# Score product of a cross-attention kernel: high and low part of a head's q on the two halves of the partitions, four products of 154 columns in place of three of 308

## The reference

```
q = layernorm(x) @ Wq            # (4, 16 heads, 1024, 64)
k, v = ctx @ Wk, ctx @ Wv        # (4, 16 heads, 154, 64)
attn = softmax(q k^T * SCALE)    # (4, 16, 1024, 154)
x = x + (attn v) @ Wo + bo
h = silu(fp4(n) @ fp4(w_gate)^T) * (fp4(n) @ fp4(w_up)^T)   # n = layernorm(x), 704 wide
x = x + fp4(h) @ fp4(w_down)^T
```

## Time and profile before

| | |
|---|---|
| Time, median of 3 runs | 921.65 us (921.07 to 922.3) |
| Profiled execution, its own time | 919.93 us |
| Its span | 918.1 us, so 1.8 us lie around it |
| Mean granted clock of TensorE | 0.982 of full speed |
| Instructions | 21443 |

### The profile page before, as it was taken

How to read it: one execution, slowest core, us unless ns; L and a number is a source line. 1 busy time by engine, 2 the same in 40 slices (tenths; PEclk the granted TensorE clock), 3 DMA queues, 4 the chain that set the end, 5 groups by cost and what they waited for, 6 DMA issues and landing times.

```text
span 918.1 us, 21443 instructions
## 1 busy us (share of the span) xinstructions
PE 839.2 (91%) x6254; PEld 801.2 (87%) x6254; DVE 707.2 (77%) x2140; ACT 524.1 (57%) x1879; POOL 544.5 (59%) x811
## 2 busy tenths in 40 slices
PE   3787899999999999989999999989999999999964
PEld 3676889999989999989988999989988999999863
DVE  5678788878777888868777888877877888887863
ACT  4554566566665556556665665656655665655521
POOL 6438577666455666654545666656554666666662
PEclk9999999999999999999999999999999999999986
DMA  7110000001010000001010000001000000000000
GB/s 239 47 28 28 7 19 13 24 13 41 14 42 13 13 25 12 23 11 47 7 36 24 7 25 12 23 16 42 13 13 19 14 24 13 14 10 12 13 6 11
DMA packets 20151, 23.22 MB, mean 25 GB/s; under 512 B 2658, under 2 KB 18250, under 8 KB 20042
## 3 DMA queue, kind: packets, MB, share of 16 engines
q1 hardware_dynamic: 20042, 21.94, 7.6%
HBM read 17.74 MB, written 4.19 MB: 24 GB/s over the span
## 4 chain that ended last, share of the span: by engine, by line
PE 64%; DVE 21%; issue 6%; ACT 5%; POOL 2%; DVEq 0%; POOLq 0%; ACTq 0%
PE ps_q L985 10%; PE ps_g L1067 9%; PE ps_s L1027 8%; PE ps_t L1037 6%; PE ps_o L1052 5%; PE ps_o L1050 5%; PE ps_o L1051 5%; DVE negmax L826 3%; DVE pT_lo L679 3%; PE ps_g L948 3%; PE ps_m L1079 3%; DVE scales L706 3%; PE ps_m L1081 2%; PE ps_m L1080 2%; PE ps_m L913 2%
## 5 line engine op out<-in xcount | busy, mean ns | idle before, releaser
L492 POOL TENSOR_TENSOR probs<-probs,rsum 128x308 f32<-128x308 f32 x256 | 180.3, 705 | 266.5 <-DVE rsum L790 259.1
L650 ACT ACTIVATE probs<-ps_s,negmax 128x154 f32<-128x154 f32 x512 | 194.7, 386 | 222.1 <-DVE negmax L826 221.0
L826 DVE TENSOR_REDUCE negmax<-ps_s 128x2 f32<-128x308 f32 x256 | 120.9, 472 | 89.0 <-PE ps_s L1027 88.4
L1050 PE MATMUL ps_o<-B_sb,pT_lo 128*128 128x256 f32 x640 | 180.5, 282 | 0.6 <-DVE x_both L881 0.6
L1052 PE MATMUL ps_o<-B_sb,pT_hi 128*128 128x256 f32 x640 | 180.4, 282 | 0.0
L1051 PE MATMUL ps_o<-B_sb,pT_hi 128*128 128x256 f32 x640 | 180.0, 281 | 0.0
L679 DVE TENSOR_TENSOR pT_lo<-ps_t,pT_hi 128x256 fp32r<-128x256 f32 (+1 forms) x256 | 122.7, 479 | 34.8 <-ACT pT_hi L544 34.3
L1067 PE MATMUL ps_g<-WGU,xqT_hi 128*128 128x352 f32 x512 | 135.5, 346 | 3.6 <-DVE B_sb L679 1.9
L1037 PE MATMUL ps_t<-ident,probs 128*128 128x128 f32 x640 | 113.8, 276 | 25.3 <-DVE pT_lo L679 22.5
L1050 PEld LDWEIGHTS ps_o<-B_sb,pT_lo 128*128 128x128 f32 x640 | 120.7, 189 | 0.9 <-issue 0.8
L1052 PEld LDWEIGHTS ps_o<-B_sb,pT_hi 128*128 128x128 f32 x640 | 121.0, 189 | 0.0
(11 more groups left out here) (157 smaller groups left out, 2198.1 us busy)
## 6 DMA issues: line engine op xcount, KB each, us to landing
xa<-in_x_dram SPq DMA_DIRECT2D x33, 128.0 KB, 2.1
xr<-in_x_dram SPq DMA_DIRECT2D x32, 128.0 KB, 2.0
out_dram<-y_xn SPq DMA_DIRECT2D x32, 128.0 KB, 1.7
W_sb<-in_L_xattn_Wk_dram SPq DMA_DIRECT2D x4, 512.0 KB, 3.6
W_sb<-in_L_xattn_Wv_dram SPq DMA_DIRECT2D x3, 512.0 KB, 3.6
probs<-in_L_xattn_Wq_dram SPq DMA_DIRECT2D x2, 512.0 KB, 7.8
Wo_sb<-in_L_xattn_Wo_dram SPq DMA_DIRECT2D x1, 1024.0 KB, 8.9
VT<-in_L_ffn_w_down_dram SPq DMA_DIRECT2D x2, 352.0 KB, 3.9
```

Source lines behind the costliest of these rows:

```text
L492: pool.tensor_tensor(unit, unit, rsum[:, 2 * u:2 * u + 2].unsqueeze(2) .to_broadcast([P, 2, M]), ALU.mult).then_inc(norm_p, 1)
L650: ins = act.activation(probs[:, h, 0:M], ps_s[k % 2][:, s * M:(s + 1) * M], ACT.Exp, bias=negmax[:, h:h + 1], accum_out=sums[:, h:h + 1])
L826: dve.tensor_reduce(negmax[:, 2 * k:2 * k + 2], ps_s[k % 2][:, 0:UM].rearrange("p (h m) -> p h m", h=2), AX_X, ALU.max, negate=True).then_ ...
L1050: pe.matmul(ps_o[:, 0:C], lo[:, j, :], w[:, 0:C], start=first, stop=False)
```

## The change

The low and the high part of q come to lie in one tile, q_sb[128, units, 2 heads, 256]. For head s, its high part is on its own 64 partitions (`mine`) and its low part on the other 64 (`other`). K's high part is written on both halves of the partitions, and K's low part on the head's own half with zeros on the other. A contraction over 128 partitions then gives q_hi x K_hi + q_lo x K_hi with K_sb[0], and q_hi x K_lo with K_sb[1], for one head and 154 columns. Per unit there are two heads and two such products, hence four matmuls, each with its own 128-column stationary operand.

```
-            pool.memset(K_sb[0][:, :, :].bitcast(F32), 0.0).then_inc(kpad_p, 1)
...
             def q_hi_part(pair, u):
-                hi_part(q_sb[0][:, u, :], ps_q[:, 0:2 * P], (q_mm, PAIRS * pair + u + 1), q_hi)
+                act.wait_ge(q_mm, PAIRS * pair + u + 1)
+                for s in range(2):
+                    ins = act.activation(q_sb[mine(s), u, s, :], ps_q[mine(s), 0:2 * P], ACT.Copy)
+                ins.then_inc(q_hi, 1)
...
                 if kind == "K":
                     act.wait_ge(k_mm, KV * b + i + 1)
-                    if isinstance(b, int) and i == 0:
-                        act.wait_ge(kpad_p, 2)
-                    for s in range(2):
-                        h = slice(D * s, D * s + D)
-                        ins = act.activation(k_dst(0, i, s), pair_of(BANKS[bank_], M)[h], ACT.Copy)
+                    for rows in (mine, other):
+                        for s in range(2):
+                            ins = act.activation(k_dst(0, i, s, rows(s)), pair_of(BANKS[bank_], M)[mine(s)], ACT.Copy)
                     ins.then_inc(k_hi, 1)
...
             def q_lo_part(pair, u):
-                lo_part(q_sb[1][:, u, :], ps_q[:, 0:2 * P], q_sb[0][:, u, :], (q_hi, PAIRS * pair + u + 1), q_lo)
+                dve.wait_ge(q_hi, PAIRS * pair + u + 1)
+                for s in range(2):
+                    ins = dve.tensor_tensor(q_sb[other(s), u, s, :], ps_q[mine(s), 0:2 * P],
+                                            q_sb[mine(s), u, s, :].bitcast(F32), ALU.subtract)
+                ins.then_inc(q_lo, 1)
...
                 if kind == "K":
                     dve.wait_ge(k_hi, KV * b + i + 1)
+                    if isinstance(b, int) and i == 0:
+                        dve.wait_ge(kpad_p, 1)
...
-                terms = ((1, 0), (0, 1), (0, 0))
-                for i, (a, b) in enumerate(terms):
-                    ins = pe.matmul(ps_s[u % 2][:, 0:UM], q_sb[a][:, u, par * P:(par + 1) * P], K_sb[b][:, u, :],
-                                    start=(i == 0), stop=(i == len(terms) - 1))
+                for s in range(2):
+                    cols = slice(s * M, (s + 1) * M)
+                    for part in (1, 0):
+                        ins = pe.matmul(ps_s[u % 2][:, cols], q_sb[:, u, s, par * P:(par + 1) * P], K_sb[part][:, u, cols],
+                                        start=(part == 1), stop=(part == 0))
                 ins.then_inc(s_mm, 1)
```

More of the change, by code:

```diff
@@ L82, in xattn_ffn_kernel @@
         xT = [sb(f"xT_{n}", [P, KT, 2 * P], F32R) for n in ("hi", "lo")]
-        q_sb = [sb(f"q_{n}", [P, PAIRS, 2 * P], F32R) for n in ("hi", "lo")]
+        q_sb = sb("q", [P, PAIRS, 2, 2 * P], F32R)
         xa = [sb(f"xa{i}", [P, C]) for i in range(2)]
@@ L287, in raw_dst, with mine, other, k_dst @@
             return dst, ps_m[:, :].rearrange("p (g k n) -> p g k n", g=2, k=KT)[:, :, :, 0:rows]
-        def k_dst(part, i, s):
-            return K_sb[part][D * s:D * s + D, 2 * i:2 * i + 2, s * M:(s + 1) * M]
+        def mine(s):
+            return slice(D * s, D * s + D)
+        def other(s):
+            return slice(D - D * s, P - D * s)
+        def k_dst(part, i, s, rows):
+            return K_sb[part][rows, 2 * i:2 * i + 2, s * M:(s + 1) * M]
         def pair_of(ps, n):
@@ L687, in take_lo @@
                     dve.wait_ge(k_hi, KV * b + i + 1)
+                    if isinstance(b, int) and i == 0:
+                        dve.wait_ge(kpad_p, 1)
                     for s in range(2):
-                        h = slice(D * s, D * s + D)
-                        ins = dve.tensor_tensor(k_dst(1, i, s), pair_of(BANKS[bank_], M)[h],
-                                                k_dst(0, i, s).bitcast(F32), ALU.subtract)
+                        ins = dve.tensor_tensor(k_dst(1, i, s, mine(s)), pair_of(BANKS[bank_], M)[mine(s)],
+                                                k_dst(0, i, s, mine(s)).bitcast(F32), ALU.subtract)
                     ins.then_inc(k_lo, 1)
```

## The result

The changed kernel takes 972.4 us (median of 4 runs, 971.2 to 973.0), against 922.0 us for the kernel before on the same chip (921.1 to 922.8). The ratio is 1.053, 95% interval 1.050 to 1.056: 50 us slower. The forecast was 944 us with a range of 915 to 970. The direction was right; the size came out at more than twice the 22 us forecast, and the time lies outside the range.

What follows compares the result with a forecast made beforehand. TensorE was taken to bound the steady part, with VectorE setting the pace in about slots 4 to 6. Terms 8.0 + 6.4 + 1.0 + 1.5 + 2.6 + 4.0 = 23.5 us on 919.93 led to 944 us, range 915 to 970.

Steps and rivals of the forecast that it cites:

- VectorE's term for q_lo: Each of 128 q_lo becomes two instructions: +6.4 us in odd tiles, +1.0 in even tiles, +1.5 before the next q product.
- TensorE, +8.0 us: Score product: four 154-column matmuls at 0.118 us replace three of 308, +0.05 us a unit, +12.8 in all, five eighths counted.
- VectorE, q_lo, price: q_lo as two 64-partition instructions on VectorE costs 0.43 us more, from +0.41 to +0.49; crossing partitions costs nothing.
- VectorE, q_lo, places: Odd tiles' slot 4 +6.4 us, even tiles' slot 5 +1.0, slots 1 and 2 +1.5, the rest hidden in VectorE idle time.
- ScalarE: Issuing q_hi twice adds 49 us of busy time to an engine at 57%, hidden except at two places counted elsewhere.
- K, +2.6 us: K's high part copied four times per job instead of two, on the chain in the rolling batches: +2.6 us, from 0 to 5.
- start, +4.0: At the kernel's start, doubled K_hi, q_hi and q_lo lie on one chain with the next q product: +4.0 us.
- The jumps: The two times the loop over the batches goes back to its top; the forecast had no term for them.
- A: Score matmuls: weight loads overlap and only columns count, 0.08 us a matmul; 922 us, down to 915; chance 9%.
- B: Score matmuls: narrow fp32r falls to the plain f32 rate, 0.26 us a matmul; about 1065 us; chance 14%.
- B2: Score matmuls: narrow fp32r at half rate, 0.13 us a matmul, +0.10 a unit; 953 us; chance 6%.
- C: All covered: loads cost 0.11 us, waits fall into VectorE idle time; 3 us of TensorE plus the start, 925 us; chance 6%.

Runs made afterwards that it cites:

- experiment 4: Kernel before, with q's low part alone issued as two instructions of 64 partitions, high part still one: 950.0 us against 924.1 (ratio 1.028).
- experiment 5: Changed kernel, with VectorE writing q's low part to the partitions it reads from: 965.4 us against 923.3 for the kernel before (ratio 1.044).
- experiment 2: Kernel before, with q's high and low parts each issued as two instructions of 64 partitions, same partitions in and out: 951.3 us against 924.1 (ratio 1.030).
- Experiment 3: Kernel before, with four ScalarE copies of K's high part per job instead of two: 929.4 us against 924.1 (ratio 1.005).
- experiments 8: Changed kernel, with the third unit of q in odd tiles made in slot 2 instead of 3: 961.6 us (ratio 1.041 to the kernel before).
- experiment 10: Kernel before, with two more waits on TensorE per unit of scores, on a semaphore long at its value: 924.9 us (ratio 1.001).
- experiments 9: Kernel before, with the third unit of q in odd tiles made in slot 2 instead of 3: 923.8 us against 923.3 (ratio 1.000).

## Why the prediction was wrong

In short: the step that failed is VectorE's term for q_lo. The sum had 8.9 us for it (6.4 + 1.0 + 1.5), and the runs show 33 (26 for the split, 7 for the crossing), since each q_lo costs 0.67 us and not 0.43, and since it is paid in slots that the prediction took for covered. The single terms:

- **TensorE, +8.0 us.** The mechanism was right: the pace is that of the weight loads, 0.11 us, and every matmul has its own load (1024 on the score line, as forecast). The term was too large (0.05 us a unit; measured 0.02), since the first step of the group is 0.07 us instead of 0.118 and the others 0.11; the attend matmul behind takes 0.04 of that back. Plain tiles show 3 us. Here the trace of 0.11 us agrees with the estimated 107 ns for 128 columns that follow from P / 1.2 in the Trainium skill, page "TensorE: Matmul & The Clock Gate", section "LDWEIGHTS (loading the stationary operand)". The estimate of +2 us that the prediction worked out from it was nearer to the measured 0.02 us a unit (5 us over 256 units) than the 12.8 I took.
- **VectorE, q_lo, price.** The step that failed first. I had the row for it: two K_lo that do not overlap. But I took 0.43 from a range of 0.41 to 0.49, worked out as the old step of 0.34 and one duration. That keeps the overlap with the instruction behind, which is lost: 0.43 + 0.42 + 0.03 = 0.89 from start to start, 0.55 more. The crossing I priced at nothing "with the doubled 0.41 as its upper end"; it costs 0.12, the overlap with the instruction ahead. Measured: 0.67.
- **VectorE, q_lo, places.** The step that failed most. I counted 6.4 us in slot 4 of odd tiles, and slot 4 grows there by 0.80 us (in the set-up tiles that make K, slot 5 by 0.77), 11 us over 14 tiles. I counted 1.0 us in slot 5 of even tiles, which is about right (0.10 a tile), 1.5 us before the next q product in slots 1 and 2, and nothing elsewhere. Slots 1 to 3 grow by 0.60 us in plain even and 0.56 in plain odd tiles, some 17 us over all tiles but those of the start and the last pair; 3 us of them are TensorE's. "The rest lie in slots with over 0.5 us of VectorE idle" was judged with the wrong price: 0.67 us does not fit into 0.5. In runs, the split of q_lo cost 26 us (experiment 4) and its crossing 7 (experiment 5), against 8.9 in the sum.
- **ScalarE** was right: experiment 2 less experiment 4 is 1 us.
- **K, +2.6 us, and start, +4.0.** Experiment 3 gives +5 us for K's copies, start included. But the start grew by 13 us in the profile, and by 12.8 and 13.5 in experiments 8 and 5. About 9 come with q's halves (8.5 and 9.2 in experiments 4 and 2); K's copies have up to 4.7, of which part is the execution's. Part is the clock: in the first 110 us it is at half for 17.0 us (mean 0.92) and was for 10.2 (0.95) before. Which of it the change brings stays open, since the start varies by 4 us without one.
- **The jumps, nothing counted, 11.8 us in the profile.** A term that was missing. What was read of the change was instructions and their times; that TensorE is idle for 1.9 to 2.1 us at each jump already was in the trace before the change. Of the 11.8 us some 3 are what such tiles grow anyway (tiles 5 and 6: 1.37 and 0.16), and 3.5 are what two falls of the clock cost in experiment 10, which takes no longer than the kernel before. Some 5 us are left for the second stops and the longer half clock. In experiments 2 and 4, with no matmul added, the stop is one, the clock falls for 3.4 us at both jumps, and the four tiles grow by 5.2 and 5.9 us: 2.2 that such tiles grow anyway and about the same two falls.
- **Rivals.** A, B and B2 were shown wrong by the distances of 0.11 us (A 0.08, B 0.26, B2 0.13). C had the right size for TensorE and the wrong one for all else; besides, its own terms, 3 us of TensorE and 4 of the start, add up to 929 us and not 925.

## What to carry to other kernels

Before halving the columns of a matmul, put its weight load beside it: with 128 stationary columns in fp32r matmuls in a row here came no faster than 0.11 us behind the first of them, so the 308 columns that went bought nothing. A change in layout has to be priced on the engines that write it: a VectorE instruction on half of the partitions costs its full columns, two on different halves do not overlap, nor does what stands behind them, and the overlap with what stands ahead (0.12 us) goes too if they write to other partitions than they read; halving the columns instead cost 0.05 us. In a loop where TensorE is busy for 94 to 97 of 100 us and VectorE hands it its operands, 0.34 us taken away from VectorE were worth nothing and 0.56 us added cost their full price and more (experiments 9 and 4), so judge "hidden" with the upper end of a price. And before a microsecond is put down to a place, compare the profiles of two kernels with the same time: here the start and the jumps differ by up to 4 us between them.

## What the runs showed of the hardware that I had not expected

- Two VectorE instructions on different halves of the partitions run one after the other to the end (0.85 us for two of 0.42), and the whole-partition instruction behind them starts 0.03 us after their end. Two on the same half or on all partitions overlap (0.48 us for two of 0.28).
- An instruction that writes to the other half loses the overlap with the one ahead: 0.39 to 0.51 us behind the same maximum, which takes 0.48. Inside a pair on different halves, which doesn't overlap anyway, the crossing adds nothing (0.43 us with and without).
- A TensorE "busy" 2.00 of 2.00 us did 19 matmuls at full clock and 10 at half. After a single stop of 1.8 to 2.4 us at a jump the clock fell to 1.2 GHz for 3.4 us in nine of 16 cases; with a second stop of 1.0 to 2.1 us behind it, in ten of ten, mostly for 6.8 us.
- At a jump TensorE starts again 1.6 to 2.1 us after the landing of a 16 KB packet of the instruction queue q8.
